# Two slots at a time on the matrix engine in the first layer's attention

## The reference, cut to what matters

```python
q = (xn @ w_q)...; k, v = split(xn @ w_kv)          # 16 heads of 64
k = concatenate([nk, k]); v = concatenate([nv, v])  # 2 null keys
q = _l2norm(q) * q_scale; k = _l2norm(k) * k_scale
sim = einsum('bhid,bhjd->bhij', q, k) * ATTN_SCALE
sim = sim + dist * slopes                           # alibi
sim = where(causal_mask, neg, sim)
attn = softmax(sim, axis=-1)
out = einsum('bhij,bhjd->bhid', attn, v)
return out.reshape(b, n, HEADS * DIM_HEAD) @ w_out
```

## Time and profile before

| | us |
|---|---|
| median of 3 runs | 2222.0 |
| the runs | 2215.68, 2222.0, 2233.71 |
| the profiled execution | 2209.62 |
| its span, first to last instruction | 2207.8 |

### The profile page before, as it was taken

How to read it: one execution, slowest core, us unless ns; L and a number is a source line. 1 busy time by engine, 2 the same in 40 slices (tenths; PEclk the granted TensorE clock), 3 DMA queues, 4 the chain that set the end, 5 groups by cost and what they waited for, 6 DMA issues and landing times. The chain is left out here.

```text
span 2207.8 us, 33163 instructions
## 1 busy us (share of the span) xinstructions
PE 1829.6 (83%) x11995; PEld 794.4 (36%) x11995; DVE 1294.9 (59%) x2140; ACT 884.0 (40%) x1393; POOL 749.8 (34%) x423
## 2 busy tenths in 40 slices
PE   1876889988889888898988886437989999899998
PEld 1455342433433334334343332225642233233233
DVE  6334765666666656667666542761156666766663
ACT  0213244444444444444444343022325455554555
POOL 1504636446355462553734565360007000000000
PEclk9898689989899898998998998659997889988898
DMA  4132100000000000000000000133321000000000
GB/s 144 53 109 56 24 5 1 7 5 6 6 1 8 5 7 2 5 8 5 1 7 1 1 1 22 39 120 87 92 68 34 25 25 15 13 25 25 25 1 20
DMA packets 52523, 61.01 MB, mean 28 GB/s; under 512 B 11386, under 2 KB 40334, under 8 KB 51470
## 3 DMA queue, kind: packets, MB, share of 16 engines
q1 hardware_dynamic: 48270, 50.52, 7.4%
q0 software_dynamic: 4096, 8.40, 1.4%
HBM read 35.09 MB, written 19.40 MB: 25 GB/s over the span
## 5 line engine op out<-in xcount | busy, mean ns | idle before, releaser
L1329 POOL TENSOR_TENSOR a_prob_sum<-a_prob_sum,a_prob 128x1024 f32<-128x1024 f32 (+2 forms) x224 | 479.6, 2141 | 260.7 <-ACT a_prob L1280 243.8
L1280 ACT ACTIVATE a_prob<-a_st,a_table 128x512 f32<-128x512 f32 (+3 forms) x640 | 367.4, 620 | 405.8 <-PE a_st L1173 245.3
L1375 DVE TENSOR_REDUCE a_maxima<-a_ring 128x16 f32<-128x512 f32 (+3 forms) x640 | 358.2, 604 | 292.3 <-PE a_ring L1104 148.8
L1766 DVE TENSOR_REDUCE a_maxima<-a_mx 128x1 f32<-128x512 f32 (+3 forms) x640 | 354.4, 605 | 166.8 <-PE a_mx L1753 125.7
L2024 ACT ACTIVATE a_prob<-a_st 128x1024 f32<-128x1024 f32 (+1 forms) x320 | 274.6, 900 | 247.0 <-PE a_st L1923 126.8
L1202 PE MATMUL a_ot<-a_prob,a_values 128*64 128x512 f32 (+3 forms) x1280 | 322.4, 584 | 60.4 <-DVE a_out_t L1444 60.4
L1753 PE MATMUL a_mx<-a_ks,a_qs 49*128 49x512 bf16 (+3 forms) x640 | 176.4, 390 | 32.2 <-DVE a_maxima L1766 29.5
L1104 PE MATMUL a_ring<-a_k_hi,a_q_hi 64*128 64x512 f16 (+3 forms) x640 | 147.8, 375 | 60.4 <-DVE a_maxima L1375 34.3
L1940 PE MATMUL a_ot<-a_prob,a_values 128*32 128x512 f32 (+3 forms) x1280 | 183.1, 628 | 0.0
L1325 POOL TENSOR_TENSOR a_prob_sum<-a_prob 128x1024 f32<-128x1024 f32 (+1 forms) x32 | 72.3, 2259 | 250.1 <-ACT a_prob L1280 118.7
L1390 DVE RECIPROCAL a_rden<-a_ring 128x512 f32<-128x512 f32 x32 | 107.4, 3356 | 53.2 <-PE a_ring L1147 52.0
(11 more groups left out here) (245 smaller groups left out, 2384.4 us busy)
## 6 DMA issues: line engine op xcount, KB each, us to landing
f_w<-in_w SPq DMA_DIRECT2D x28, 256.0 KB, 2.9
expert_in<-zeros SPq DMA_DIRECT2D x5, 1024.0 KB, 10.8
f_rows<-expert_in SPq DMA_DIRECT2D x16, 256.0 KB, 3.6
a_values<-values_all SPq DMA_DIRECT2D x8, 512.0 KB
expert_out<-f_result SPq DMA_DIRECT2D x16, 256.0 KB, 2.5
shared_w<-in_w SPq DMA_DIRECT2D x12, 256.0 KB, 2.9
parts<-p_part_t SPq DMA_DIRECT2D x6, 512.0 KB, 2.7
a_table<-in_head_table SPq DMA_DIRECT2D x16, 140.5 KB, 2.1
```

The source lines that it names most:

```text
L1280: e = act.activation(prob[:, s % NPROB, a, c0:QW], ps_st[s % 2][:, a, c0:QW], ACT.Exp, bias=table[x][:, a, at:at + 1])
L1329: pool.tensor_tensor(into[:, :, c0:QW], into[:, :, c0:QW], here[:, :, c0:QW], ALU.add).then_inc(added, 2 if r == TPQ - 2 else 1)
L1375: dve.reduce_max(maxima[:, qt // TPQ, a, qt % TPQ, at:at + count], bank[:, 0:hi - lo].rearrange("p (w k) -> p w k", k=WINDOW), AX_X).then_ ...
L1766: dve.reduce_max(own.maxima[:, qt // TPQ, a, qt % TPQ, n:n + 1], bank[:, 0:hi - lo], AX_X).then_inc(done, 1)
```

## The change

`slots0` now builds its entries two slots at a time. The units of `one` stay at their slots, those of `two` of an even slot are put behind those of the odd slot, and the ring's banks are handed out in the new order: `one` of n, `one` of n + 1, `two` of n, `two` of n + 1. All engines read that list. In TensorE's `step`, per two slots: `one` of n, scores of n and n + 1, `one` of n + 1, weighted sums of n - 2 and n - 1, then both `two` lists. Each scores group and each weighted sum waits for the same exponential as before.

```diff
-    for n in range(2 * NS0 + (4 if last else 0)):
+    total = 2 * NS0 + (4 if last else 0)
+
+    def ahead_of_sums(n):
+
         x, s = divmod(n, NS0)
...
+        return one
+
+    def behind_sums(n):
+
...
-        out.append((n, x, s, one, two))
+        return two
+
+    for n in range(0, total, 2):
+        ones = [ahead_of_sums(n), ahead_of_sums(n + 1)]
+        twos = behind_sums(n) + behind_sums(n + 1)
+        out.append((n, *divmod(n, NS0), ones[0], []))
+        out.append((n + 1, *divmod(n + 1, NS0), ones[1], twos))
...
                 for n, x, s, one, two in slots0(first, last)[0]:
-                    slots = i * (2 * NS0) + n
-                    if x < 2:
+                    for unit in one:
+                        put(unit, base, 2 * i + unit.what[0], i)
+                    if n % 2 == 0 and x < 2:
                         if s == 0:
                             pe.wait_ge(null_loaded[x], 16 * i + 16)
-                        if SLOTS0[s][1] == 0:
-                            pe.wait_ge(row_loaded[SLOTS0[s][0]], 64 * i + 32 * x + 32)
-                        if n >= 2 or not first:
-                            pe.wait_ge(exp_done, slots - 1)
-                        scores(x, s)
-                    for unit in one:
-                        put(unit, base, 2 * i + unit.what[0], i)
-                    if (n >= 2 or not first) and n < 2 * NS0 + 2:
-                        px, ps = divmod(n - 2, NS0)
-                        pe.wait_ge(exp_done, slots - 1)
-                        if SLOTS0[ps][1] == 0 and not (first and n == 2):
-                            qb = SLOTS0[ps][0]
-                            pe.wait_ge(ot_read, i * (2 * NQB) + NQB * px + qb)
-                        weighted(px % 2, ps)
+                        for m in (n, n + 1):
+                            if SLOTS0[m % NS0][1] == 0:
+                                pe.wait_ge(row_loaded[SLOTS0[m % NS0][0]], 64 * i + 32 * x + 32)
+                            if m >= 2 or not first:
+                                pe.wait_ge(exp_done, begun + m - 1)
+                            scores(x, m % NS0)
+                    if n % 2 == 1:
+                        for m in (n - 3, n - 2):
+                            if (m < 0 and first) or m >= 2 * NS0:
+                                continue
+                            px, ps = divmod(m, NS0)
+                            pe.wait_ge(exp_done, begun + m + 1)
+                            if SLOTS0[ps][1] == 0 and not (first and m == 0):
+                                pe.wait_ge(ot_read, i * (2 * NQB) + NQB * px + SLOTS0[ps][0])
+                            weighted(px % 2, ps)
                     for unit in two:
                         put(unit, base, 2 * i + unit.what[0], i)
```

More of the change, by code:

```diff
@@ L875, in slots0 @@
         more = not tail and not (last and x == 1)
-        one, two = [], []
+        one = []
         if not tail:
@@ L891, in slots0 @@
             one.append(ring.put("den", (x, DEN_AT0[s])))
+        return one
+    def behind_sums(n):
+        x, s = divmod(n, NS0)
+        tail = x == 2
+        more = not tail and not (last and x == 1)
+        unborn = first and x == 0 and s < 4
+        two = []
         if more and s < QK_UNITS0:
@@ L1207, in step @@
                 base = base0(i)
+                begun = i * (2 * NS0)
                 for n, x, s, one, two in slots0(first, last)[0]:
-                    slots = i * (2 * NS0) + n
-                    if x < 2:
+                    for unit in one:
+                        put(unit, base, 2 * i + unit.what[0], i)
+                    if n % 2 == 0 and x < 2:
                         if s == 0:
                             pe.wait_ge(null_loaded[x], 16 * i + 16)
-                        if SLOTS0[s][1] == 0:
-                            pe.wait_ge(row_loaded[SLOTS0[s][0]], 64 * i + 32 * x + 32)
-                        if n >= 2 or not first:
-                            pe.wait_ge(exp_done, slots - 1)
-                        scores(x, s)
-                    for unit in one:
-                        put(unit, base, 2 * i + unit.what[0], i)
-                    if (n >= 2 or not first) and n < 2 * NS0 + 2:
-                        px, ps = divmod(n - 2, NS0)
-                        pe.wait_ge(exp_done, slots - 1)
-                        if SLOTS0[ps][1] == 0 and not (first and n == 2):
-                            qb = SLOTS0[ps][0]
-                            pe.wait_ge(ot_read, i * (2 * NQB) + NQB * px + qb)
-                        weighted(px % 2, ps)
+                        for m in (n, n + 1):
[13 more added lines that the diff above has]
+                            weighted(px % 2, ps)
                     for unit in two:
```

## The result

The changed kernel takes 2091.9 us (median of 4 runs, 2078.6 to 2108.2) against 2218.8 of the kernel before (now the median of four runs); the ratio is 0.9435 with an interval of 0.9332 to 0.9537. The gain is 5.7%, where 2.1% was forecast: the direction was right, the forecast gain less than half of what came. The profiled execution took 2098.6 us, 111 less than the profiled one of before.

The account below looks back on a forecast made before the run. TensorE, busy 973.8 of the stage's 1120.0 us, was taken as the bound, its matmuls and 146 idle us movable. Gains 29 + 33, less 15 and 1, clock 0: 46 us, ratio 0.979, 2176 us; range 2140 to 2216.

Parts of the forecast that it names:

- (e): Granted clock in the stage, mean 0.93: no change taken; bounds 24 us of gain, or a third more lost.
- the clock rises as well: Rival: halved row-end waits keep slots 1 to 6 at 2.4 GHz; 24 us more, 70 in all, 2152 us; chance 0.15.
- (c): Slots 9 to 16: slot 11's wait stays, later waits grow; 2.2 us worse a head pair, 15 us in all.
- (d): Slot 29's fourth maxima: wait for the negated maxima goes from 2.31 to 2.4 us; 1 us worse in all.
- (a): TensorE's changes between matmul forms, about 0.10 us each: fewer after the change, 29 us of gain; bounds 13 and 38.
- (b): Row ends: weighted sums' waits for VectorE shrink and move to the maxima; 4.0 us gained a pair, 33 us in all.
- only the waits go: Rival: weighted sums back to back are no faster; 16 us fewer, 30 us of gain, 2192 us; chance 0.14.
- VectorE keeps the time: Rival: VectorE is late at the ring after every row end; only 8 us of gain, 2214 us; chance 0.13.
- slower: Rival: transposes in slots 13 to 16 wait for VectorE and the clock drops; 29 us slower, 2251 us; chance 0.08.
- the five units through three banks: Slots 13 to 16, cause in the slower rival: values and four transposes come together; 8 us a pair, plus 5 for clock.

Follow-up runs that it names:

- e5: Kernel before plus extra matmuls, results thrown away, in front of the waiting weighted sums at slots 2, 6, 14 and 26; ratio 0.9890.
- e8: Changed kernel with VectorE's inverse roots in two parts, the maxima of slot 10 between them; ratio 0.9352 to the kernel before.
- e10: Kernel before with GpSimd's additions cut to 8 columns (output wrong, only the time of use); ratio 0.9685.
- e11: Changed kernel with GpSimd's additions cut to 8 columns (output wrong, only the time of use); ratio 0.9267 to the kernel before.
- e1: Changed kernel with the odd slot's maxima put between the two weighted sums, scores still in twos; ratio 0.9651 to the kernel before.
- e3: Changed kernel's list of units on all engines, but TensorE in its old slot-by-slot order; ratio 0.9894 to the kernel before.
- e4: Kernel before with each row's first weighted sum issued one slot later, just ahead of the second; ratio 0.9810.

## Why the prediction was wrong

The idle time of TensorE was forecast to fall by 33 - 15 - 1 = 17 us and fell by 43. Its busy time was to fall by some 25 and fell by 73, of which some 28 are clock and some 36 form changes (both estimates).

The lost clock by place, added up over the eight pairs, in us (the stage's first and last microseconds are left out):

| slots | before | changed | e5 | e8 |
|---|---|---|---|---|
| 0 to 7 | 26 | 5 | 12 | 8 |
| 10 and 11 | 16 | 20 | 9 | 0 |
| 12 to 17 | 33 | 9 | 14 | 2 |
| all others | 2 | 0 | 7 | 0 |

A stretch of the kernel before, around slots 0 to 3 of the pair behind the one that the forecast read:

```profile
820.00:840.00 20.00, 15.98 (x107) 6.92 (x107) 10.37 (x13) 6.55 (x15) 4.94 (x4) 0.83 0.08 19
```

- **(e) the clock, forecast 0: the step that failed most.** It said that the clock fell behind the waits of slots 11 to 16, "Those waits stay, so I take no change". Lost clock went from 82.6 to 39.8 us. Two things were wrong. A third of the loss lay in slots 0 to 7, around the row ends of slots 1 to 6, which this part of the forecast left out; e5, which fills the waits there, halves it. The one pair that was read the earlier trace rows is quiet at that place, the next one has a clock of 0.83. And in slots 12 to 16 the waits did not stay: they fell from 6.3 to 4.5 us a pair, the longest from 2.7 to 2.0, and the loss fell with them. The rival "the clock rises as well" had the direction and the price (24 us; about 28 by e5's rate), with a chance of 0.15. Its mechanism, the stretches around slots 1 to 6, is half of what came.
- **(c) slots 9 to 16, forecast 15 us worse.** Measured 7.6 us of waits a pair against 8.1, where 1.0 more was forecast, and by two errors that partly cancel. Slot 11 was to stay as it was, since "as many scores, sums and projections as now" come before it; fewer do, and it went from 1.77 to 3.14 us. In the slots behind it the wait for the reciprocal at slot 13 came as walked (2.02 against 2.2), but the one behind the negation was walked with the addition at 2.53 us, and it took 0.71 at that place (698.74). I took as a duration what was mostly a wait for GpSimd.
- **(d) slot 29, forecast 2.4 us.** Measured 0.73, for the same reason: 0.44 in place of 2.29. That is 11 us over the seven pairs. e10 and e11 put the whole effect of GpSimd's additions at 25 us of the difference. The forecast had no such term, and neither did a rival; that the additions fell into better places is luck.
- **(a) form changes, forecast 29 us.** Mechanism right, size some 36: the 67 double slots that the kernel before and the changed one both show at full clock and without idle time are 0.22 us shorter on the mean, times 160 (e10 and e11 give 0.24 in 90). e1, which undoes a part, gives some 28. Two pieces were mis-sized: the sum-to-sum hand-over saves 0.10 + 0.05, since the second's first weight load is hidden too, and two projection groups together saved 0.20 where e3 shows them, not 0.10. The rule of the Trainium skill (TensorE: Matmul & The Clock Gate, Part 3, The mechanism) that no load is hidden between equal row groups was weighed rightly: 0.91, not 1.01.
- **(b) row ends, forecast 33 us.** The mechanism is right: the waits moved to the ring as said. The sizes are mixed: 1.17 us for 1.2 at slots 26 and 27, but 1.23 for 0.5 at slots 5 and 6 and 1.27 for 0.95 at slots 1 and 2. That is 2.9 us gained a pair, not 4.0, and some 24 us of idle time in all with the last pair. e4, which has only this, takes away 27.5 us of idle time and gives 39 us of stage with its share of the clock.
- The terms do not add up one by one, because the clock multiplies each. In order of the edits: list alone 19 us, scores in twos 46, sums in twos 51; together 116.

The rivals: "only the waits go" is out by the 0.91 us hand-over and by e1, "VectorE keeps the time" and "slower" by the result; the five units through three banks cost 2.0 us at one place and at most 0.9 at the others.

## What to carry to other kernels

Where an engine alternates between two kinds of matmul, read the start-to-start times at each change of form: 0.10 us a change, two changes in most of 160 double slots, was worth pairing. When a wait of TensorE is removed, price the clock too, and look at every place where the granted clock falls, in more than one pair: in e4 27.5 us of idle time brought 39 us of stage, in e8 12 us brought 25. When an order changes, count again what stands between a wait and the work that it waits for; slot 11's wait nearly doubled unseen. And before a duration of VectorE goes into a walk, look whether GpSimd was running beside it; an addition with both inputs in SBUF may be five times shorter at another moment.

## What was not expected of the hardware

- Matmuls thrown away made a kernel faster: e5 has 26 pairs of 512 columns more in each pair of heads and is 1.1% faster (0.9890 [0.982, 0.996]).
- The same VectorE addition of 272 columns takes 0.44 or 2.29 us, by whether one of GpSimd's is running.
- A shorter VectorE chain (e8) removed 12 us of idle time and 23 us of lost clock: the waits of 3.1 us, once in some 127 us, had come with a granted clock of 0.83 in the 20 us around (670 to 690), in an engine that was otherwise busy.
